# Causal convolution folded into four TensorE products on tap-weighted projection weights

## What is computed

```python
xz = x @ in_proj_w                       # 128 -> 2 * 256
xb, zb = jnp.split(xz, 2, axis=-1)
xb = lax.conv_general_dilated(xb, conv_w, window_strides=(1,), padding=[(D_CONV - 1, 0)],
        dimension_numbers=('NWC', 'WIO', 'NWC'), feature_group_count=D_INNER) + conv_b
xb = jax.nn.silu(xb)
...
x_dbl = xb @ x_proj_w
...
h = dc * h + ic                          # scan over positions, 16 states
```

## Time and profile before

| | |
|---|---|
| median of three runs | 3630.56 us (3628.31 to 3631.08) |
| the profiled execution | 3629.41 us |
| its span | 3627.6 us |
| first half (pipeline over batches) | to some 2020 us |
| second half (not touched) | from there on |

### The profile page before, as it was taken

How to read it: one execution, slowest core, us unless ns; L and a number is a source line. 1 busy time by engine, 2 the same in 40 slices (tenths; PEclk the granted TensorE clock), 3 DMA queues, 4 the chain that set the end, 5 groups by cost and what they waited for, 6 DMA issues and landing times. The chain is left out here.

```text
span 3627.6 us, 53483 instructions
## 1 busy us (share of the span) xinstructions
PE 2920.3 (81%) x15912; PEld 2143.3 (59%) x15912; DVE 2813.8 (78%) x4814; ACT 1952.1 (54%) x4744; POOL 888.7 (24%) x590
## 2 busy tenths in 40 slices
PE   2387889888988888888889867888888888888876
PEld 1164566556655665566556546666666666667665
DVE  3999999999999999999997246666666666666664
ACT  3466768676867686767675423333333333333332
POOL 0443333333333333333332000011111111111111
PEclk6588999999999999999999989999999999999998
DMA  2000000000000000000000020000000000000000
GB/s 103 8 4 14 17 19 3 19 16 19 3 19 19 16 3 19 19 16 3 16 17 17 12 74 10 17 16 16 16 16 16 16 16 16 16 16 16 16 8 11
DMA packets 49771, 64.31 MB, mean 18 GB/s; under 512 B 3584, under 2 KB 36416, under 8 KB 49184
## 3 DMA queue, kind: packets, MB, share of 16 engines
q1 hardware_dynamic: 47392, 54.93, 4.7%
q10 hardware_dynamic: 2304, 8.46, 0.6%
HBM read 41.78 MB, written 21.60 MB: 17 GB/s over the span
## 5 line engine op out<-in xcount | busy, mean ns | idle before, releaser
L789 POOL TENSOR_TENSOR acc<-acc,zz 128x1024 f32<-128x1024 f32 x256 | 608.4, 2376 | 1006.1 <-DVE h L1104 958.7
L1104 DVE TENSOR_TENSOR_SCAN h<-dec,u 128x1024 f32<-128x1024 f32 x256 | 585.4, 2287 | 13.2 <-issue 4.9
L918 PEld LDWEIGHTS bank<-one_sb,hid 128*128 128x128 f32 x4096 | 481.4, 193 | 30.9 <-issue 17.3
L918 PE MATMUL bank<-one_sb,hid 128*128 128x128 f32 x4096 | 483.3, 276 | 14.6 <-ACT hid L654 14.6
L866 PE MATMUL bank<-S,pick_sb 96*128 96x512 bf16 x512 | 209.4, 414 | 254.0 <-DVE zz L1116 141.0
L158 POOL TENSOR_SCALAR n_ve<-n_mv 128x4 f32<-128x4 f32 x96 | 54.4, 567 | 1360.2 <-DVE n_mv L141 1360.2
L622 ACT ACTIVATE dec<-dt,aneg 128x512 f32<-128x512 f32 (+1 forms) x512 | 341.4, 723 | 63.7 <-DVE h L1104 48.0
L1116 DVE TENSOR_TENSOR zz<-h,bank 128x1024 f32<-128x1024 f32 x256 | 312.5, 1221 | 10.5 <-PE bank L866 0.3
L866 PEld LDWEIGHTS bank<-S,pick_sb 96*128 96x128 bf16 x512 | 50.0, 98 | 447.5 <-DVE zz L1116 204.8
L1097 DVE TENSOR_TENSOR u<-dtx,bank 128x1024 f32<-128x1024 f32 x256 | 309.9, 1211 | 0.4 <-PE bank L866 0.3
L654 ACT ACTIVATE hid<-banks,one_sb 128x512 f32<-128x512 f32 x304 | 208.4, 691 | 106.5 <-PE bank L918 64.5
(11 more groups left out here) (265 smaller groups left out, 6975.8 us busy)
## 6 DMA issues: line engine op xcount, KB each, us to landing
kv_dram<-Gs ACTq DMA_DIRECT2D x16, 516.5 KB, 3.1
kvl<-kv_dram SPq DMA_DIRECT2D x16, 516.5 KB, 3.6
xs<-in_x SPq DMA_DIRECT2D x16, 256.0 KB, 2.8
x<-in_x SPq DMA_DIRECT2D x16, 256.0 KB, 2.9
x_dram<-x SPq DMA_DIRECT2D x16, 256.0 KB, 2.1
h_dram<-hT SPq DMA_DIRECT2D x16, 256.0 KB, 2.0
h<-h_dram SPq DMA_DIRECT2D x16, 256.0 KB, 2.6
x2s<-x_dram SPq DMA_DIRECT2D x16, 256.0 KB, 2.7
```

The costliest lines, as they stand in the source:

```text
L789: pool.tensor_tensor(acc[:, :, :], acc[:, :, :], zz[:, k % 2, :, :], ALU.add)\
L918: last = pe.matmul(bank1(f"down{e}")[:, j * D:(j + 1) * D], hid[:, e % 2, f, j * P:(j + 1) * P], w2[:, e, f, :], start=(f == 0), stop=(f = ...
L1104: dve.tensor_tensor_scan(h[:, :, :].rearrange("p g t -> p (g t)"), dec[:, k % 2, :, :].rearrange("p g t -> p (g t)"), u[:, :, :].rearrange ...
```

## The change

Before the batches, eight matrices are made once: `tapw[:, k, :]` is the x half of `inw` with each column scaled by that channel's tap k. DVE scales the identity by the taps (eight tensor_scalar of 128x128 into h), PE spreads the scales over the partitions with a product of ones (eight matmuls into banks 2 and 3), DVE multiplies them into `inw` (two tensor_tensor of 128x512). For each batch, `in_x` becomes four accumulating matmuls, on hT shifted by one position each; hT has three zero columns in front. `silu_x` reads PSUM, half by half, with the bias, in ACT's slots 9 and 10, ahead of the slot's Relus. `keep_x`, `convolve`, xpad and cv go. `in_x(1)` moves on PE within slot 9, behind all ups. `x_proj` stays in slot 12. The two halves of x now free bank 7 with xc_ok.

```diff
-            hT = sb("hT", [P, T])
-            xpad = sb("xpad", [P, G, PAD + T])
-            pos = xpad[:, :, PAD:]
-            cv = sb("cv", [P, G, T])
-            ax = cv
+            hT = sb("hT", [P, PAD + T])
+            pos = sb("pos", [P, G, T])
+            ax = sb("ax", [P, G, T])
...
-            freed.update({f"x{g}": (NXT, xraw, g + 1) for g in range(G)})
+            freed.update({f"x{g}": (NXT, xc_ok, g + 1) for g in range(G)})
...
-                    def keep_x(g, n):
+                    def silu_x(g, n):
                         act.wait_ge(*in_done(n, g + 1))
-                        act.wait_ge(*conv(n, 0))
-                        act.wait_ge(*dt_ok(n, 0))
-                        act.activation(xpad[:, g, PAD:], bank1(f"x{g}"), ACT.Copy).then_inc(xraw.sem, 1)
-
-                    def silu_x(n):
-                        act.wait_ge(*conv(n, G))
                         act.wait_ge(*acc0(n, 0))
                         act.wait_ge(*dtx_ok(n, 0))
-                        act.activation(xc[:, :, :], cv[:, :, :], ACT.Silu).then_inc(xc_ok.sem, 1)
+                        act.activation(xc[:, g, :], bank1(f"x{g}"), ACT.Silu, bias=convb[:, g:g + 1])\
+                            .then_inc(xc_ok.sem, 1)
...
-                            if n is not None and slot == 11:
-                                silu_x(n)
+                            if n is not None and slot - 1 in XIN:
+                                silu_x(XIN[slot - 1], n)
...
+                    for g in range(G):
+                        for k in range(TAPS):
+                            last = pe.matmul(banks[2 + g][:, k * P:(k + 1) * P], ones[:, :],
+                                             h[:, g, k * P:(k + 1) * P], start=True, stop=True)
+                        last.then_inc(tap_rows, 1)
+                    pe.wait_ge(tap_ok, G)
...
-                        pe.matmul(bank1(f"x{g}"), inw[:, g * P:(g + 1) * P], hT[:, :],
-                                  start=True, stop=True).then_inc(in_done.sem, 1)
+                        for k in range(TAPS):
+                            last = pe.matmul(bank1(f"x{g}"), tapw[:, k, g * P:(g + 1) * P], hT[:, k:k + T],
+                                             start=(k == 0), stop=(k == PAD))
+                        last.then_inc(in_done.sem, 1)
...
-                                if slot in XIN:
-                                    in_x(XIN[slot], n, s)
+                                if slot == 8:
+                                    in_x(0, n, s)
...
+                                if slot == 9:
+                                    in_x(1, n, s)
...
+                    for g in range(G):
+                        for k in range(TAPS):
+                            dve.tensor_scalar(h[:, g, k * P:(k + 1) * P], ident, convw[:, g, k:k + 1], None,
+                                              ALU.mult).then_inc(tap_cols, 1)
+                    for g in range(G):
+                        dve.wait_ge(tap_rows, g + 1)
+                        cols = slice(g * P, (g + 1) * P)
+                        dve.tensor_tensor(tapw[:, :, cols], banks[2 + g][:, :].rearrange("p (k c) -> p k c", k=TAPS),
+                                          mid(inw[:, cols], TAPS), ALU.mult).then_inc(tap_ok, 1)
...
-                                if slot in CONV:
-                                    convolve(CONV[slot], n)
```

More of the change, by code:

```diff
@@ L346, in adaln_depth2 @@
             aneg = sb("aneg", [P, G, NS])
+            tapw = sb("tapw", [P, TAPS, DI])
             xs = sb("xs", [P, J, D])
             ga = sb("ga", [P, D])
-            hT = sb("hT", [P, T])
-            xpad = sb("xpad", [P, G, PAD + T])
-            pos = xpad[:, :, PAD:]
-            cv = sb("cv", [P, G, T])
-            ax = cv
+            hT = sb("hT", [P, PAD + T])
+            pos = sb("pos", [P, G, T])
+            ax = sb("ax", [P, G, T])
             zs = sb("zs", [P, G, T])
@@ L410, in adaln_depth2 @@
             L3 = Norm(sb, sig, "n3", EPS_MOD)
-            (in_done, xraw, zsilu, conv, xc_ok, xdbl, dtr_ok, s_hi, s_mid, s_rem, s_remb, s_lo, s_ok, dtps, dtabs,
+            tap_cols, tap_rows, tap_ok = (sem(n) for n in ("tap_cols", "tap_rows", "tap_ok"))
+            (in_done, zsilu, xc_ok, xdbl, dtr_ok, s_hi, s_mid, s_rem, s_remb, s_lo, s_ok, dtps, dtabs,
              dtexp, dtln, dt_ok, dtx_ok, acc0, bb, cbc, dec_ok, u_ok, scan, z_ok, accum, yz_ok, oproj, ao_ok,
-             x1_ok, chainA) = (sig(n, p) for n, p in (
-                 ("in_done", 4), ("xraw", 2), ("zsilu", 2), ("conv", 2), ("xc_ok", 1), ("xdbl", 1), ("dtr_ok", 1),
+             x1_ok) = (sig(n, p) for n, p in (
+                 ("in_done", 4), ("zsilu", 2), ("xc_ok", 2), ("xdbl", 1), ("dtr_ok", 1),
                  ("s_hi", 1), ("s_mid", 1), ("s_rem", 1), ("s_remb", 1), ("s_lo", 1), ("s_ok", 1), ("dtps", 2),
@@ L417, in adaln_depth2 @@
                  ("cbc", NS), ("dec_ok", 2 * NS), ("u_ok", NS), ("scan", NS), ("z_ok", NS), ("accum", NS),
-                 ("yz_ok", 1), ("oproj", 1), ("ao_ok", 1), ("x1_ok", 1), ("chainA", G * (TAPS - 1))))
+                 ("yz_ok", 1), ("oproj", 1), ("ao_ok", 1), ("x1_ok", 1)))
             (logits, lshift, lexp, gw, gturn, gT_ok, b2ps, b2_ok, up, hid_ok, down, taken, fsum, fgate, x2_ok,
@@ L554, in modulate1 @@
                         act.wait_ge(*in_done(n, 0))
-                        act.activation(hT[:, :], bank1("turn1"), ACT.Identity, scale=modc[:, 0, n, 1:2],
+                        act.activation(hT[:, PAD:], bank1("turn1"), ACT.Identity, scale=modc[:, 0, n, 1:2],
                                        bias=modc[:, 0, n, 0:1]).then_inc(L1.out.sem, 1)
-                    def keep_x(g, n):
+                    def silu_x(g, n):
                         act.wait_ge(*in_done(n, g + 1))
-                        act.wait_ge(*conv(n, 0))
-                        act.wait_ge(*dt_ok(n, 0))
-                        act.activation(xpad[:, g, PAD:], bank1(f"x{g}"), ACT.Copy).then_inc(xraw.sem, 1)
-                    def silu_x(n):
-                        act.wait_ge(*conv(n, G))
                         act.wait_ge(*acc0(n, 0))
                         act.wait_ge(*dtx_ok(n, 0))
-                        act.activation(xc[:, :, :], cv[:, :, :], ACT.Silu).then_inc(xc_ok.sem, 1)
+                        act.activation(xc[:, g, :], bank1(f"x{g}"), ACT.Silu, bias=convb[:, g:g + 1])\
+                            .then_inc(xc_ok.sem, 1)
                     def silu_z(g, a):
@@ L596, in magnitude @@
                         act.wait_ge(*dtps(n, g + 1))
-                        act.wait_ge(*xc_ok(n, 1))
+                        act.wait_ge(*dt_ok(n, 0))
                         act.activation(pos[:, g, :], bank1(f"dt{g}"), ACT.Relu, bias=dtb[:, g:g + 1])
@@ L729, in step @@
                             if n is not None:
-                                if slot in XIN:
-                                    keep_x(XIN[slot], n)
                                 if slot == 12:
@@ L776, in _ @@
                 def _(pool):
-                    pool.memset(xpad[:, :, 0:PAD], 0.0).then_inc(init, 1)
+                    pool.memset(hT[:, 0:PAD], 0.0).then_inc(init, 1)
                     pool.memset(thirty[:, :], 1.0 / 32).then_inc(init, 1)
@@ L824, in _ @@
                     pe.wait_ge(w_low, E0)
+                    pe.wait_ge(init, 4)
+                    pe.wait_ge(tap_cols, G * TAPS)
+                    for g in range(G):
[4 more added lines that the diff above has]
+                    pe.wait_ge(tap_ok, G)
                     def turn1(n, s):
@@ L834, in in_x @@
                         free1(pe, f"x{g}", s)
-                        pe.matmul(bank1(f"x{g}"), inw[:, g * P:(g + 1) * P], hT[:, :],
-                                  start=True, stop=True).then_inc(in_done.sem, 1)
+                        for k in range(TAPS):
+                            last = pe.matmul(bank1(f"x{g}"), tapw[:, k, g * P:(g + 1) * P], hT[:, k:k + T],
+                                             start=(k == 0), stop=(k == PAD))
+                        last.then_inc(in_done.sem, 1)
                     def in_z(g, a, s):
                         free1(pe, f"z{g}", s)
-                        pe.matmul(bank1(f"z{g}"), inw[:, (G + g) * P:(G + g + 1) * P], hT[:, :],
+                        pe.matmul(bank1(f"z{g}"), inw[:, (G + g) * P:(G + g + 1) * P], hT[:, PAD:],
                                   start=True, stop=True).then_inc(in_done.sem, 1)
                     def x_proj(n, s):
-                        pe.wait_ge(*xc_ok(n, 1))
+                        pe.wait_ge(*xc_ok(n, G))
                         free1(pe, "xdbl", s)
@@ L1051, in _ @@
                                           ALU.subtract).then_inc(w_low, 1)
[L1052 to L1069, removed]
+                    for g in range(G):
[7 more added lines that the diff above has]
+                                          mid(inw[:, cols], TAPS), ALU.mult).then_inc(tap_ok, 1)
```

(4 more changed lines are left out.)

1 line of the change is left out of this document (removed).

## The result

The changed kernel takes 3686.5 us (median of 4 runs, 3683.3 to 3692.9) against 3630.8 us (3628.3 to 3633.8) for the kernel before: 1.0155 times its time, 95% interval 1.0138 to 1.0173. The forecast was 3688. The profiled execution after is one of 3688.3 us.

The account below looks back on a forecast made before the run. PE, full in slots 9 to 15, was taken to set dt through ACT, so its added matmuls cost time: 3629.4 + 53.5 + 3.8 = 3686.7, with the runs' median 1.15 higher, so 3688 us; range 3660 to 3714.

Parts of the forecast that it names:

- What bounds: Up to dt, the chain PE, ACT, dt decides: a late PE costs in full, DVE early at dt wins nothing.
- The price of a matmul: Six more fp32 matmuls of 512 columns a batch in slots 8 and 9, 0.86 us each: 5.16 us.
- C_8, C_9 and C_10: PE's spreads of C for slots 8 to 10 in the walked step: foretold at 951.0, about 957.7 and 964.1.
- The kinds of step: Fourteen full steps get longer: four by 2.75 us, seven by 4.1, three by 4.6; sum 53.5 us.
- the seven walked: Seven steps like the one walked through slots 8 to 15: each 5.16 - 1.09 = 4.1 us longer.
- I take 0.86 for all six: All six added matmuls in slots 8 and 9 priced at full clock, the half-clock stretch no longer than before.
- The wait of 0.56 behind a Relu: PE's wait on ACT in three long half-clock steps, taken to vanish, so these lose 4.6 us.
- Once: Outside the full steps: setup about +6.3 us, step -1 +0.5, step 0 -3; together +3.8.
- A: DVE bounds and its time is won: fifteen steps shorter by 5.6 us, 3553 us in all; chance 5%.
- B: Mostly absorbed: PE at full clock through slots 8 to 16, steps 1 to 2.3 us longer, 3648 to 3667; 15%.
- C: ACT's extra table loads delay a dec or Relu: 18 to 36 us more, 3706 to 3724; chance 16%.
- The signs: Steps 122 to 125 us; DVE waits 5 to 10 at spreads, dt 1 to 3 for Ln; PE above 88%.

Follow-up runs that it names:

- e9: The changed kernel with two more products for each half, their values written over (ten more matmuls a batch than before): 3747.1 us, 1.0287 of the kernel before.
- e10: The changed kernel with the first tap left out, three products for each half in place of four: 3662.9 us, 1.0065 of the kernel before.
- e1: The changed kernel with one tap product for each half in place of four, everything else as changed: 3608.4 us, 0.9919 of the kernel before.
- e2: The kernel before with DVE's convolution cut to its last tap, PE and ACT as they were: 3611.3 us, 0.9936 of the kernel before.
- e3: The kernel before, convolution kept on DVE, with each in_x matmul issued four times: 3708.5 us, 1.0200 of the kernel before.
- e4: The changed kernel with in_x(0) moved behind the downs of slot 8 on PE: 3644.2 us, 1.0021 of the kernel before.
- e5: The changed kernel with Relu in place of Silu for x, which needs no table load: 3681.3 us, 1.0144 of the kernel before.
- e7: e6 with the downs of slot 10 ahead of that slot's last ups on PE: 3610.2 us, 0.9954 of the kernel before.
- e6: The kernel before, half 0 convolved on DVE, half 1 by four PE products, in_x blocks behind downs and ups: 3618.4 us, 0.9971 of before.
- e8: The kernel before, convolution whole, with in_x(0) behind slot 8's downs and keep_x(0) behind its Relus: 3656.1 us, 1.0083 of the kernel before.

## Why the prediction was right

**What bounds: right.** In this order, PE's extra time in slots 8 to 15 reaches the end of the step in full (e9, e10), while DVE's removed time does not (e1, e2, and e3 from the other side). The reading that decided it was the pair of the earlier trace rows, not the shares of the earlier trace rows. DVE's 95% there was no bound: about a fifth of what was taken from it came back as time. By the section "Identifying the Most-Contended Engine" of the Trainium skill's page "Perfetto Trace Analysis", TensorE's 59% of weight loads would have left it room. The slope of 1.0 says that over these slots, in this order, it has none.

**The price of a matmul: right.** 0.86 us each: three more make 2.58, and the block of four lasts 3.67 with eight records where the clock is full. In the step above, of the kind walked, C_8, C_9 and C_10 came within 0.2 us of the times foretold.

**The kinds of step: the size was off, twice.** From slot 8's first instruction on DVE to dt it took 52.5 us before (53.4 in the three slow steps). Steps of full clock have +2.8 after (forecast 2.75). The others have +4.3 to +5.8 (forecast 4.1 and 4.6). The first of the fourteen, which the sum took as one of the seven walked, is 6.6 us longer: there PE waits 3.22 us for hT, and the block behind it lasts 6.66 us. Two terms were too small:
- "I take 0.86 for all six": `in_x(0)` is one of the blocks that PE enters at half clock, and a longer block at its front has more of it there.

```profile
847.68 3.67 PE L836 MATMUL bank<-hT,tapw 128*128 128x512 f32 x8 [1.40 <-ACT hT L554]
...
1095.01 6.58 PE L836 MATMUL bank<-hT,tapw 128*128 128x512 f32 x8 [1.40 <-ACT hT L554]
```

  In this case, 6.58 against 3.67, the clock comes back only as the block ends (0.56 granted over 1095.0 to 1101.6). e4, which puts `downs` there, has no such stretch.
- The wait of 0.56 behind a Relu was taken to appear in the three slow steps only, and to go there. It stands in all fourteen, 8.0 us. It had been covered by the waits for DVE before B_10 and C_10: e2, which only takes DVE's work away, shows it 15 times. e5 shows that the loads don't cause it, and e7 removes it by letting the `downs` of slot 10 go first, which free the hidden buffer that the Relu writes.

The 2.8 of the full-clock steps is in part luck. The new 0.56 is in it, and it came out right because C_10 was only 2.2 us later than before (23.68 for 21.47 after slot 8's first instruction), 0.5 less than 5.16 - 2.43. Together the 14 steps took 58.6 us where the sum had 53.5.

**Once: right in sum, not in parts.** +2.9 against +3.8. The first dt is 8.3 us later for a forecast of 6.8. Of this, 1.0 lies ahead of the setup, in code that both kernels have (DVE's last work there starts at 43.52 for 42.52). Setup took 5.8 on DVE (48.34 to 54.16) for 6.3, where the prediction's own three items add up to 6.1. Step -1 cost some 1.5 for the +0.5 taken: the first `in_x` block has a granted clock of 0.55 (6.69 us), and the second waits 0.78 for the first silu. Step 0 gave back 5.4 for 3.

```profile
60.55 6.69 PE L836 MATMUL bank<-hT,tapw 128*128 128x512 f32 x8 [1.01 <-ACT hT L554]
68.01 3.70 PE L836 MATMUL bank<-hT,tapw 128*128 128x512 f32 x8 [0.78 <-ACT xc L561]
72.58 1.96 PE L849 MATMUL bank<-xc,one_sb 128*128 128x512 f32 x4 [0.87 <-ACT xc L561]
```

So 58.6 + 2.9 = 61.5 is 4.2 above the forecast's 57.3, and the tail behind the last full step is 3 us shorter (3686.3 - 1895.7 = 1790.6 against 3627.6 - 1834.2 = 1793.4). That code is untouched and varies by as much between other kernels here. The agreement of 3688 with 3686.5 is therefore closer than the terms of the sum earn, and the last 3 us of it are luck.

**The rivals.** A (DVE's time is won) fell with e1 and e2. B (mostly absorbed) fell: the clock is full in slot 8 of as few steps as before. In another order it is nearly so: e4's step is 0.8 us longer than before, a little under B's 1 to 2.3. C (ACT's loads on top) had its two signs, the 1.28 on dec and the 0.56 on the Relu, and was still wrong: e5 takes the loads away and gains 5.4 us, not 18 to 36. A wait that a view shows is not yet time of the step; the next wait may stand behind it. **The signs** came nearly as foretold: steps of 123.3 to 125.8 us from slot 8 to slot 8 for 122 to 125, DVE 6.6 us a step on the spreads for 5 to 10, dt 1.6 for 1 to 3. But the last was no sign of a late PE: e1, without the extra matmuls, has the same 22.7 us of it. And the spreads are waited for at zz of slots 9 to 12 alone, not at u or up to slot 15. PE's share of the pipeline is 87.8% where it was to be above 88%.

## What to carry to other kernels

Find where in a pipeline step each engine has no slack, and price a shift of work by that place; an engine's share of the whole step does not show it (DVE 95%, about a fifth of its removed time was won; PE 86%, its added time cost in full). Then ask for the order: of two blocks that an engine can take in either order, the one whose input is there goes first, where it fills the wait and keeps the clock up, worth 42 to 49 of 56 us here. Splitting the work between both engines (e6, e7) beat either extreme. The same order alone lost (e8): it only moved PE's wait to a place where the half clock behind it hit the bound, and in e6 PE's own added products fill that place.

## What was not expected of the hardware

An engine that arrives 2.60 us early can be worse than one that is just in time: in e8 TensorE was at full clock (1.00) over 833.0 to 838.5, stood 2.60 us before 841.68, and had a granted clock of 0.50 over the next 4.72 us, in which it was busy throughout. In e6, which has 2.58 us more work for TensorE at this place, the wait and the half clock behind it are gone. Beyond that, the code behind the last full step, which the edits leave all but untouched, differed by up to 15 us from kernel to kernel (1786 to 1802), and nothing here explains it.
